# Two-layer attention kernel on one core: a shorter loading stage, statistics and wo spread over the first row, one transpose moved to another bank

## The reference

```python
x = L0_attn_x                                   # (8, 512, 256) f32
for layer in (0, 1):
    xn = layernorm(x)                           # over the last axis, eps 1e-5, no scale
    s = attention(xn)                           # layer 0: 16 heads of 64, rope, causal; layer 1: 16 heads of 16
    g = silu(ffn(xn))                           # layer 0: int weights times 1/127, hidden 768; layer 1: 8 experts
    x = x + s * g
return x
```

## Time and profile before

| | |
|---|---|
| median of 3 runs | 1987.37 us (1984.23 to 1990.66) |
| the profiled execution | 1987.64 us |
| its span | 1985.8 us |
| PE busy | 1847.7 us, 93% |
| DVE / ACT / POOL busy | 71% / 60% / 30% |
| mean granted TensorE clock | 0.982 |

### The profile page before, as it was taken

How to read it: one execution, slowest core, us unless ns; L and a number is a source line. 1 busy time by engine, 2 the same in 40 slices (tenths; PEclk the granted TensorE clock), 3 DMA queues, 4 the chain that set the end, 5 groups by cost and what they waited for, 6 DMA issues and landing times. The chain is left out here.

```text
span 1985.8 us, 32448 instructions
## 1 busy us (share of the span) xinstructions
PE 1847.7 (93%) x11568; PEld 1411.5 (71%) x11568; DVE 1411.8 (71%) x2881; ACT 1191.2 (60%) x2809; POOL 605.4 (30%) x958
## 2 busy tenths in 40 slices
PE   1999999999999999999999959998799999999997
PEld 1887888878778888878888758887455555555553
DVE  5785885885885867858858854443677777777773
ACT  3665675674664765756756755554466666666664
POOL 0354353443543443543534523222100110011012
PEclk9999999999999999999999989999799999999999
DMA  6111111211111111111101157332733444353421
GB/s 234 42 34 33 44 43 27 49 44 33 43 33 44 41 25 46 41 33 43 44 25 41 43 170 286 120 115 74 202 106 101 133 146 120 112 163 93 132 70 43
DMA packets 104047, 162.34 MB, mean 82 GB/s; under 512 B 11984, under 2 KB 53456, under 8 KB 103376
## 3 DMA queue, kind: packets, MB, share of 16 engines
q1 hardware_dynamic: 103368, 159.75, 28.1%
q10 hardware_dynamic: 520, 0.52, 0.1%
HBM read 80.55 MB, written 46.14 MB: 64 GB/s over the span
## 5 line engine op out<-in xcount | busy, mean ns | idle before, releaser
L1584 DVE TENSOR_REDUCE nm<-ps 128x1 f32<-128x512 f32 x512 | 338.4, 686 | 120.3 <-PE ps L1463 117.6
L1677 ACT ACTIVATE pt<-pst 128x512 f32<-128x512 f32 x512 | 290.2, 599 | 194.1 <-PE pst L1472 191.6
L805 POOL TENSOR_SCALAR pr<-pr,rinv 128x128 f32<-128x128 f32 (+3 forms) x512 | 263.2, 533 | 374.8 <-DVE rinv L693 374.8
L573 ACT ACTIVATE pr<-sc,nmax 128x128 f32<-128x128 f32 (+3 forms) x512 | 268.1, 527 | 143.4 <-DVE nmax L682 141.9
L682 DVE TENSOR_REDUCE nmax<-sc 128x1 f32<-128x128 f32 (+3 forms) x512 | 223.3, 485 | 76.5 <-PE sc L409 76.4
L1463 PE MATMUL ps<-kb,qb 96*128 96x512 f32 x512 | 237.1, 465 | 27.5 <-DMA kb<-z_scratch 15.3
L811 POOL TENSOR_TENSOR qk<-ra,rb 128x256 f32<-128x256 f32 x256 | 182.9, 735 | 206.4 <-DVE rb L704 170.9
L1463 PEld LDWEIGHTS ps<-kb,qb 96*128 96x128 f32 x512 | 97.9, 191 | 185.5 <-DVE nm L1584 123.6
L1472 PE MATMUL pst<-qb,kb 128*128 128x512 f32 x512 | 207.0, 406 | 3.4 <-ACT pt L1677 2.9
L421 PE MATMUL w<-ident,pr 128*128 128x128 f32 x1280 | 170.6, 280 | 25.7 <-DVE rb L704 19.8
L1419 POOL TENSOR_TENSOR so<-so,g_sb 128x256 f32<-128x256 f32 x32 | 23.5, 733 | 535.4 <-DVE so L1621 535.4
(11 more groups left out here) (213 smaller groups left out, 4227.6 us busy)
## 6 DMA issues: line engine op xcount, KB each, us to landing
k<-k SPq DMA_DIRECT2D x256, 128.0 KB, 2.2
z_scratch<-zt SPq DMA_DIRECT2D x96, 256.0 KB, 2.5
qb<-z_scratch SPq DMA_DIRECT2D x64, 192.0 KB, 3.8
kb<-z_scratch SPq DMA_DIRECT2D x64, 192.0 KB, 4.0
raw<-in_w SPq DMA_DIRECT2D x16, 640.0 KB, 6.1
raw<-in_w SPq DMA_DIRECT2D x8, 704.0 KB, 4.2
xa<-in_x SPq DMA_DIRECT2D x2, 2048.0 KB, 13.8
x<-in_x SPq DMA_DIRECT2D x8, 512.0 KB, 4.0
```

The source lines that it names most:

```text
L573: act.activation(pr[:, h, SOFF[i]:SOFF[i] + (i + 1) * P], sc[:, bank, at:at + (i + 1) * P], ACT.Exp, bias=nmax[:, h, i:i + 1], accum_out=r ...
L805: pool.tensor_scalar(p, p, rinv[:, h, i:i + 1], 1.0, ALU.mult, ALU.mult).then_inc(scaled, 1)
L1584: dve.tensor_reduce(nm[:, g % 2, i, h:h + 1], ps[:, i % 2, :], AXX, ALU.max, negate=True).then_inc(max_done, 1)
L1677: act.activation(pt[:, g % 2, h, i, :], pst[:, i % 2, :], ACT.Exp).then_inc(exp_done, 1)
```

## The change

- The loading stage loads only both halves of wqkv, x rows 0 and 1 (straight into the tile `x` that layer 0 uses), rope, wg, wu, wd and the bias, in this order. Its statistics cover 8 tiles instead of 32. x row 0 and row 1 are not loaded again.
- The statistics of rows 2 to 7 are computed during row 0, in six parts on DVE: one after each of the pairs 1 to 6. Their x comes in three transfers of two rows each into a buffer `xs`. SP issues the first at the start of layer 0, the second in the turn hp = 2 of its loop when 8 statistics are done, the third in the turn hp = 4 when 16 are done. The square root and reciprocal for these rows stand in row 1.
- wo comes in two halves during row 0; ACT rounds a half after pair 1 and after pair 4, and DVE subtracts after pair 2 and after pair 5. Row 0's output projection waits for all of it.
- In the first pair of each row, `turn_p(n, 0, 2)` writes `po` instead of bank 3, and waits for `o_lo_done` instead of `rope_mult`.
- The norm of the next row is done one tile at a time, after the pairs 1 to 4, instead of four tiles after the first pair.

```diff
@@ load_layer0, SP
-                half = B * NT // 2
                 for i in range(2):
                     sp.dma_start(wq_raw[:, i, :], wq[:, i, :]).then_inc(wq_in[i], 16)
-                    sp.dma_start(xa[:, i * half:(i + 1) * half, :], xt[:, i * half:(i + 1) * half, :]).then_inc(x_in[i], 16)
-                sp.dma_start(wo_raw[:], io.wo0.rearrange("(c p) n -> p c n", p=P)).then_inc(wo_in, 16)
+                sp.dma_start(c.x[:], xt[:, 0:FIRST, :]).then_inc(x_in, 16)
+                sp.dma_start(c.rope[:], io.rope).then_inc(small_in, 16)
...
@@ load_layer0, ACT
-                act.wait_ge(wo_in, 16)
-                act.copy(c.wo_hi[:], wo_raw[:]).then_inc(hi_done, 1)
...
-                act.wait_ge(aggr_done, B * NT)
+                act.wait_ge(aggr_done, FIRST)
...
@@ layer0, SP
-                sp.dma_start(x[:, 0:NT, :], x_dram[:, 0]).then_inc(x_loaded, 16)
+                xt = io.x.rearrange("b (t p) c -> p (b t) c", p=P)
+                sp.dma_start(xs[:], xt[:, 2 * NT:4 * NT, :]).then_inc(xs_in, 16)
+                wo = io.wo0.rearrange("(c p) n -> p c n", p=P)
+                sp.dma_start(wo_raw[:], wo[:, 0:NP0 // 2]).then_inc(wo_in, 16)
...
                         for h in range(2):
                             copy_half(b * NP0 + hp, h)
-                        if hp == 0 and b < B - 1:
+                        if hp == 0 and 0 < b < B - 1:
                             load_x(b + 1)
+                        if hp == 3 and b == 0:
+                            sp.wait_ge(wo_lo_done, 1)
+                            sp.dma_start(wo_raw[:], wo[:, NP0 // 2:]).then_inc(wo_in, 16)
+                        if hp in (2, 4) and b == 0:
+                            sp.wait_ge(stats0_done, hp * NT)
+                            sp.dma_start(xs[:], xt[:, (hp + 2) * NT:(hp + 4) * NT, :]).then_inc(xs_in, 16)
...
@@ layer0, PE, pair
                         elif j < 2:
                             pe.wait_ge(pt_b_copied, 3 * n - 1 + j)
+                        elif first:
+                            pe.wait_ge(o_lo_done, n + 1)
                         elif slot == "project":
                             pe.wait_ge(rope_mult, NT * (n + 2) + 3)
...
-                        turn_p(n, 0, j)
+                        turn_p(n, 0, j, out=po if first and j == 2 else None)
...
@@ layer0, ACT
+                def round_wo(part):
+                    act.wait_ge(wo_in, 16 * part + 16)
+                    half = slice(part * NP0 // 2, (part + 1) * NP0 // 2)
+                    act.copy(c.wo_hi[:, half], wo_raw[:]).then_inc(wo_hi_done, 1)
...
+                    if b == 1:
+                        act.wait_ge(aggr0_done, REST)
+                        act.activation(dev0[:], aggr0[:, :, 1], ACT.Sqrt, bias=c.eps[:]).then_inc(dev0_done, 1)
                     act.activation(spare[:], c.ident[:, 0:1], ACT.Exp)
...
                     for hp in range(1, NP0 - 2):
                         pair(b, hp)
+                        if b == 0 and hp in (1, 4):
+                            round_wo(hp // 4)
...
@@ layer0, DVE
+                def rest_stats(r):
+                    dve.wait_ge(xs_in, 16 * (r // 2) + 16)
+                    for i in range(NT * r, NT * r + NT):
+                        dve.bn_stats(stats0[:, i, :], xs[:, i % (2 * NT), :]).then_inc(stats0_done, 1)
+                    for i in range(NT * r, NT * r + NT):
+                        dve.wait_ge(stats0_done, i + 1)
+                        dve.bn_aggr(aggr0[:, i, :], stats0[:, i, :]).then_inc(aggr0_done, 1)
...
+                def rest_wo(part):
+                    half = slice(part * NP0 // 2, (part + 1) * NP0 // 2)
+                    dve.wait_ge(wo_hi_done, part + 1)
+                    dve.tensor_tensor(c.wo_lo[:, half], wo_raw[:], c.wo_hi[:, half].bitcast(F32), ALU.subtract).then_inc(wo_lo_done, 1)
...
                     pair(b, 0, first=True)
-                    if not last:
-                        norm(b + 1)
                     for hp in range(1, NP0 - 2):
                         pair(b, hp)
+                        if hp <= NT and not last:
+                            norm(b + 1, range(hp - 1, hp))
+                        if b == 0:
+                            rest_stats(hp - 1)
+                            if hp in (2, 5):
+                                rest_wo(hp // 5)
                     pair(b, NP0 - 2, slot=None if last else "turn_x")
+                    if b == 0:
+                        rest_stats(NP0 - 3)
...
```

More of the change, by code:

```diff
@@ L115, in load_layer0 @@
     c.bo = m.sb("bo", [P, C])
+    c.x = m.sb("x", [P, 2 * NT, C])
+    c.eps = m.sb("eps", [P, 1])
     with ExitStack() as ctx:
         t = Mem(nc, ctx)
-        xa = t.sb("xa", [P, B * NT, C])
         wq_raw = t.sb("wq_raw", [P, NC, NP0 * PC0])
-        wo_raw = t.sb("wo_raw", [P, NP0, C])
         wg_int, wu_int, wd_int = (t.sb(n, [P, NC * F0], I32) for n in ("wg_int", "wu_int", "wd_int"))
[L122 to L126, removed]
+        FIRST = 2 * NT
+        stats = t.sb("stats", [P, FIRST, 6])
+        aggr = t.sb("aggr", [P, FIRST, 2])
+        dev = t.sb("dev", [P, FIRST])
+        eps = c.eps
+        x_in = t.sem("x_in")
         wq_in = [t.sem(f"wq_in{i}") for i in range(NC)]
@@ L130, in load_layer0 @@
         wd_in = t.sem("wd_in")
-        wo_in = t.sem("wo_in")
         small_in = t.sem("small_in")
@@ L195, in _ @@
                     dve.tensor_tensor(o[:, :, 2 * D0:], v[:, :, 2 * D0:], h[:, :, 2 * D0:], ALU.subtract).then_inc(lo_done, 1)
[L196 to L205, removed]
+                    if half == 0:
+                        dve.wait_ge(x_in, 16)
+                        for i in range(FIRST):
+                            dve.bn_stats(stats[:, i, :], c.x[:, i, :]).then_inc(stats_done, 1)
+                        for i in range(FIRST):
+                            dve.wait_ge(stats_done, i + 1)
+                            dve.bn_aggr(aggr[:, i, :], stats[:, i, :]).then_inc(aggr_done, 1)
+                dve.wait_ge(aggr_done, FIRST)
+                dve.tensor_copy(c.mean[:, 0:FIRST], aggr[:, :, 0]).then_inc(rstd_done, 1)
                 dve.wait_ge(dev_done, 1)
-                dve.reciprocal(c.rstd[:], dev[:]).then_inc(rstd_done, 1)
+                dve.reciprocal(c.rstd[:, 0:FIRST], dev[:]).then_inc(rstd_done, 1)
                 dve.wait_ge(rstd_done, 2)
-                dve.wait_ge(lo_done, 2 * NC + 1)
+                dve.wait_ge(lo_done, 2 * NC)
 def layer0(nc, m, c, io):
@@ L219, in layer0 @@
         t = Mem(nc, ctx)
-        x = t.sb("x", [P, 2 * NT, C])
+        x = c.x
+        REST = (B - 2) * NT
+        xs = t.sb("xs", [P, 2 * NT, C])
+        wo_raw = t.sb("wo_raw", [P, NP0 // 2, C])
+        stats0 = t.sb("stats0", [P, REST, 6])
+        aggr0 = t.sb("aggr0", [P, REST, 2])
+        dev0 = t.sb("dev0", [P, REST])
         xn = t.sb("xn", [P, NT, C])
@@ L250, in layer0 @@
         x_loaded = t.sem("x_loaded")
+        xs_in = t.sem("xs_in")
+        stats0_done = t.sem("stats0_done")
+        aggr0_done = t.sem("aggr0_done")
+        mean0_done = t.sem("mean0_done")
+        dev0_done = t.sem("dev0_done")
+        rstd0_done = t.sem("rstd0_done")
+        wo_in = t.sem("wo_in")
+        wo_hi_done = t.sem("wo_hi_done")
+        wo_lo_done = t.sem("wo_lo_done")
         x1_stored = t.sem("x1_stored")
@@ L410, in scores, with turn_p @@
                                       start=False, stop=(m > 0)).then_inc(s_done, 1)
-                def turn_p(n, h, j):
+                def turn_p(n, h, j, out=None):
                     if j == 2 - 2 * h:
@@ L420, in turn_p @@
                     for kt, i, at in tile:
-                        mm = pe.transpose(w[:, 1 - h + j, at:at + P],
+                        mm = pe.transpose((w[:, 1 - h + j] if out is None else out)[:, at:at + P],
                                           pr[:, h, SOFF[i] + kt * P:SOFF[i] + (kt + 1) * P], c.ident[:])
@@ L544, in row @@
                     pe.wait_ge(o_lo_done, n + 1)
+                    if b == 0:
+                        pe.wait_ge(wo_hi_done, 2)
+                        pe.wait_ge(wo_lo_done, 2)
                     out_project(0, early)
@@ L595, in take_o, with take_p @@
                     act.copy(ho_hi[:, bass.ds(hp, 1), :].rearrange("p o t -> p (o t)"), po[:, :]).then_inc(o_hi_done, 1)
-                def take_p(n):
-                    for turn, (bank, at, width) in enumerate(((3, 1024, 256), (1, 0, 512), (2, 512, 512))):
+                def take_p(n, first):
+                    for turn, (src, at, width) in enumerate(((po if first else w[:, 3], 1024, 256), (w[:, 1], 0, 512), (w[:, 2], 512, 512))):
                         act.wait_ge(p_turned, 6 * n + turn + 1)
-                        act.copy(pt[:, 0, at:at + width], w[:, bank, 0:width]).then_inc(pt_a_copied, 1)
+                        act.copy(pt[:, 0, at:at + width], src[:, 0:width]).then_inc(pt_a_copied, 1)
                 def pair(b, hp, slot="project", turn=True, first=False):
```

(32 more changed lines are left out.)

1 line of the change is left out of this document (removed).

## The result

The changed kernel takes 1993.19 us (median, 1990.33 to 1995.51), the kernel before 1988.31 in the runs beside it: a ratio of 1.0025 with a 95% interval of 1.0019 to 1.0031. It is 4.9 us slower. That is less than the 0.3% that the prediction called the smallest change to be told, yet the interval lies above 1, so a small loss is shown. 1988.0 was predicted, 0.6 above the 1987.37 it started from. The profiled execution has a span of 1991.7.

The account below looks back on a forecast made before the run. PE was taken as the bound, busy nearly all the time, with its waits in layer 0 and its late start deciding. Terms -14.9 - 11.3 + 0 + 4.8 + 21.8 = +0.4 on the span of 1985.8 gave 1988.0 us, range 1979 to 1997.

Parts of the forecast that it names:

- loading stage: Ahead of layer 0: stage ends at 25.3 instead of 36.3 us and x's second load goes, together -14.9 us.
- first pairs: First pair of all eight rows: PE resumes earlier and the clock stays up, gaining 11.3 us.
- the rest of rows 1 to 7: Norm tiles after pairs 1 to 4 of a row fit DVE's idle time: 0.
- DVE's work ahead of pairs 2, 4, 6, 7: Row 0: statistics and wo remainders delay PE after pairs 1, 3, 5 and 6, +4.8 us in all.
- two pauses and the clock after them: Row 0, ahead of pairs 3 and 5: PE stands 8.9 us each, plus 2.0 each for the lowered clock, +21.8.
- the wait in the SP queue: Row 0, turns hp = 2 and 4: copies of k leave only after the statistics and behind the x transfer, +21.8 us.
- (b): Row 0: PE doesn't feel the SP wait, only DVE's work after pairs 2 and 4 shows; 1970 us, chance 0.06.
- (c): Row 0: `bn_stats` takes twice as long beside POOL, +8, 1996 us; chance 0.07.
- (d): First pair of all rows: the clock falls although the pause is in pieces, +8, 1996 us; chance 0.12.
- (a): Row 0: the copies of k pass the x transfer, a pause is 5.6 us, 1981.4 in all; chance 0.15.

Follow-up runs that it names:

- e1_order: The changed kernel with the next x transfer and its wait moved one turn later in SP's loop, behind the copies of k: 1971.55 us, ratio 0.9916.
- f3_spread: The changed kernel with row 0's added DVE work put where DVE is idle and each x transfer behind the copies it could delay: 1966.54 us, ratio 0.9881.
- f2_pair6: e1_order with wo's second half rounded after pair 3 and its remainder taken after pair 4 instead of 5: 1970.51 us, ratio 0.9906.
- e4_po_norm: The kernel before with only the first pair's third transpose into the outputs' bank and the norm split over four pairs: 1976.92 us, ratio 0.9938.

## Why the prediction was right, point by point

| term | predicted | profiled execution |
|---|---|---|
| loading stage (start of row 0's gate projection, 50.91 to 36.45) | -14.9 | -14.5 |
| first pairs, from the first scores to the first `weigh`: row 0 (23.20 to 21.32) and rows 1 to 7 (158.87 to 149.64 together) | -11.3 | -1.9 - 9.2 = -11.1 |
| the rest of rows 1 to 7 (whole rows: 968.39 to 960.62) | 0 | +1.5 |
| DVE's work ahead of pairs 2, 4, 6, 7 (each from `weigh` to `weigh`) | +4.8 | 0.8 + 0.8 + 3.8 - 0.2 = +5.2 |
| two pauses and the clock after them | +21.8 | 20.0 + 4.5 = +24.5 |
| layer 1, from the last matmul of layer 0 on (826.2 to 827.1) | 0 | +1.0 |
| span | +0.4 | +5.9 |

The prediction's mechanism stands: the wait in the SP queue ate the gains, as e1_order shows by taking it away alone. Of its rivals, (b) falls with the 24.2 us of waits. (c), `bn_stats` twice as slow beside POOL, falls too: its 24 instructions took 404 to 426 ns in row 0, as at other places (mean 426 in layer 0 of the kernel before). (d) falls for this kernel, since no first pair of its trace lowered the clock; row 6 of f3_spread shows that it can happen. (a), the copies passing the transfer, is wrong in its price (5.6 us a pause) and right in that the copies don't wait for the whole transfer. The measured terms add up to 6.6, 0.7 more than the change of the span. Row 0 is 27.1 us longer (140.4 to 167.4) where its terms add up to 27.8; pair 5 of the kernel before took 13.80 us from `weigh` to `weigh` where its neighbours take 12.92, behind a wait for its copy of k, and the pause swallowed that. The 1.0 us in layer 1, whose code is the same, I can't assign.

Four sizes were off. A pause was 10.0 and not 8.9. The part ahead of the transfer was shorter than I said: the next instruction starts 0.31 us after a norm tile's start there, not 0.66, so the transfer left 1.8 us after PE had stopped, not 2.5. But from the issue of the transfer to the landing of the copies it took 8.3 us (99.02 to 107.32) where the prediction had 5.2 + 1.2 = 6.4. I had let only head 0's copies pass behind the transfer; in the trace four copies were in flight with it and all of them landed late. The clock after a pause cost 2.7 and 1.8 us (from the scores to `weigh` 12.23 and 11.32, where the steady pair takes 9.54), 4.5 in place of 4.0.

Pairs 2 and 4 became 0.8 us longer (13.71 from `weigh` to `weigh` where it was 12.91 and 12.92), 0.5 of it as a pause, and not 1.1, for the same reason: with 0.31 for the norm tile the prediction's own sum gives 0.8. Pair 6 lost more, 3.8 in place of 1.9: 2.2 in the pause and 1.6 because the clock fell after it. The prediction had the half of wo's remainder at 1.14 us, from an instruction with POOL idle beside it; there it took 1.74, and POOL was at work in its first part. And it counted the clock after the two long pauses only. f2_pair6 shows that with 0.80 us there the clock stays up.

The gain in the first pairs came out as forecast, 11.1 for 11.3. What was missing is a small cost in every row: from the gate projection to the first scores rows 1 to 7 take 22.2 us in place of 22.0, and a steady pair 12.95 in place of 12.92. e4_po_norm, which has the first-pair parts alone, has 22.0 and 12.92, so the cost comes with the other parts; which of them, and how, no run shows.

On the port pair that the Trainium skill describes (page "SBUF — State Buffer"), the row that I read, 0.66 us per tile, was four tiles beside POOL's scaling. A single tile at the end of a pair took 403 to 409 ns in all rows of after, POOL's scaling under way or not, POOL's four scalings beside the tile of pair 1 took 2.13 us (2.11 in the earlier trace rows), and PE's waits for POOL in the first pairs stay at 0.6 us or less. For the norm tiles the rule decided nothing. For the wo remainder, which reads two operands from SBUF, the traces agree with a hold of one engine by the other: 1.50 and 1.74 us in after in place of 1.14, and in f3_spread POOL's scalings 1.1 us longer beside it. That the port pair is the cause, no run shows by itself.

## What to carry to other kernels

A queue that issues in program order, as SP's does here, turns a wait for a far event into a wait for everything written behind it: before a transfer with a wait is put into a loop, look up when the entries behind it used to be issued. Work moved off the start into a steady loop is free only where its engine is idle and nothing stands behind it; two kernels with the same instructions differ here by 1.3%, by order alone (1993 and 1967 us). And a pause cost more than its length where the clock fell after it: taking 1.7 us off the pause of 2.5 us in pair 6 also kept the clock up.

## What the runs showed that I had not expected

A 128 KB copy inside SBUF that lands 2.2 us after its issue when alone needed 6.9 us behind a transfer of 1024 KB and 4.9 behind 512 KB (medians of four in flight together, which alone need 2.4); the first half of the transfer lengthened PE's pause by 3.5 us and the second by 1.8. The clock was down after pauses of 10, 8, 4.7 and 2.5 us (0.50 to 0.57 over the 4 to 6 us of work that followed in after), and it stayed up after the pause of 2.0 us in e1_order and those of 2.0, 1.4 and 0.8 us in f2_pair6. In the kernel before the same pause of 2.47 us lowered it in five rows and left it up in three. In f3_spread it fell once, in a first pair with pauses of 0.75 and 0.83 us, while pauses of 0.73 and 0.76 us in the same first pair of after left it up. So the length of a pause alone doesn't decide it.
